# Attention in one fused network: a small product that gathers softmax denominators is given another place in TensorE's order

## The reference, cut to what matters

```python
q = jnp.einsum('qdh,bcd->bhcq', Q, x) * sq
k = jnp.einsum('qdh,bcd->bhcq', K, x) * sq
v = jnp.einsum('vdh,bcd->bhcv', V, x) * sv
att = jnp.einsum('bhcq,bhCq->bhcC', q, k) / d_query
att = jnp.where(causal, att, -jnp.inf)
p = jax.nn.softmax(att, axis=-1)
y = jnp.einsum('bhcC,bhCv->bhcv', p, v)
z = jnp.einsum('dvh,bhcv->bcd', W, y) * (...)
```

## Time and profile before

| | |
|---|---|
| median of three runs | 2140.64 us (2138.8 to 2143.95) |
| the profiled execution, its own time | 2142.65 us |
| its span in the profile | 2140.9 us |
| TensorE busy | 1889.4 us, 88% of the span |
| VectorE, ScalarE, GpSimd busy | 64%, 50%, 55% |
| attention, 650 to 1890 us of the span | TensorE busy 1216.50 of 1240 us |

### The profile page before, as it was taken

One profiled execution on the slowest core, in us unless ns is written; L12 is line 12 of the kernel. 1 busy time (PEld: TensorE's weight loads), 2 busy tenths in 40 slices (PEclk: granted clock), 3 DMA queues, 4 the chain that ended last, 5 costly groups with the idle time before them and its releaser, 6 DMA issues. The chain is left out here.

```text
span 2140.9 us, 39708 instructions
## 1 busy us (share of the span) xinstructions
PE 1889.4 (88%) x12071; PEld 1430.0 (67%) x12072; DVE 1361.5 (64%) x3652; ACT 1079.1 (50%) x2250; POOL 1177.9 (55%) x1159
## 2 busy tenths in 40 slices
PE   5864999999589999999999999999999999973870
PEld 3553888888466677777777677777777777753750
DVE  7884334434467777657777656777656777653763
ACT  5331333333455556646655646655646655522760
POOL 4364223223216666636687836687836687835782
PEclk9856999999899999999999999999999999977995
DMA  9853433333332111111221111121112111122979
GB/s 335 268 188 119 89 52 49 52 52 49 77 92 56 53 55 49 54 32 53 54 77 41 48 33 53 51 53 47 48 27 59 48 52 51 39 94 70 205 129 257
DMA packets 215682, 177.33 MB, mean 83 GB/s; under 512 B 85442, under 2 KB 200727, under 8 KB 214880
## 3 DMA queue, kind: packets, MB, share of 16 engines
q1 hardware_dynamic: 177904, 138.78, 22.1%
q0 software_dynamic: 28656, 27.61, 8.4%
q10 hardware_dynamic: 8960, 8.92, 1.2%
HBM read 95.05 MB, written 80.72 MB: 82 GB/s over the span
## 5 line engine op out<-in xcount | busy, mean ns | idle before, releaser
L952 POOL TENSOR_TENSOR c_den_late<-c_den_late,c_p 128x512 f32<-128x512 f32 (+3 forms) x384 | 409.9, 1068 | 227.6 <-ACT c_p L1267 183.5
L1267 ACT ACTIVATE c_p<-PS 128x512 f32<-128x512 f32 (+3 forms) x768 | 343.6, 491 | 196.1 <-PE PS L2483 119.0
L2452 PE MATMUL PS<-c_k,c_q 128*128 128x512 f32 (+2 forms) x768 | 289.3, 377 | 18.1 <-DVE c_max L1838 6.7
L2495 PE MATMUL PS<-c_p,c_vh 128*64 128x256 f32 (+3 forms) x3072 | 292.5, 333 | 0.0
L2475 PE MATMUL PS<-c_q,c_k 128*128 128x512 f32 (+2 forms) x768 | 283.7, 373 | 1.8 <-DMA c_q<-c_mr 1.2
L888 POOL DMA_INDIRECT acc<-b_y,b_tok x71 | 110.5, 1557 | 272.8 <-ACT b_y L1137 241.7
L2495 PEld LDWEIGHTS PS<-c_p,c_vh 128*64 128x64 f32 x3072 | 194.6, 137 | 96.0 <-issue 38.1
L2476 PE MATMUL PS<-c_q,c_k 128*128 128x512 f32 (+2 forms) x768 | 258.4, 348 | 0.0
L1258 ACT ACTIVATE c_q<-PS 64x512 fp32r<-64x512 f32 x256 | 151.0, 590 | 208.6 <-PE PS L2439 205.4
L1845 DVE CUSTOM_DVE_ANT_0 PS<-PS,c_maskq,c_max 128x128 f32<-128x128 f32 (+3 forms) x256 | 143.1, 559 | 105.5 <-PE PS L2452 71.5
L1838 DVE TENSOR_REDUCE c_max<-PS 128x1 f32<-128x512 f32 x256 | 175.5, 685 | 54.2 <-PE PS L2452 53.6
(11 more groups left out here) (304 smaller groups left out, 4009.7 us busy)
## 6 DMA issues: line engine op xcount, KB each, us to landing
c_vh<-c_v SPq DMA_DIRECT2D x64, 256.0 KB, 3.2
c_rrow<-rden SPq DMA_DIRECT2D x63, 256.0 KB, 3.6
routed<-b_empty SPq DMA_DIRECT2D x32, 289.0 KB, 10.2
d_xe<-routed SPq DMA_DIRECT2D x32, 289.0 KB, 4.0
b_xt<-routed SPq DMA_DIRECT2D x71, 130.0 KB, 2.1
b_w12T<-in_w12T_dram SPq DMA_DIRECT2D x16, 512.0 KB, 13.9
d_acc<-acc SPq DMA_DIRECT2D x16, 512.0 KB, 9.0
c_st_hi<-wqk_split SPq DMA_DIRECT2D x48, 128.0 KB
```

Of the source, the lines that this page charges most:

```text
L952: pool.tensor_tensor(den[:, off:], den[:, off:], p, ALU.add).then_inc(s_cPa, 1)
L1267: act.activation(c_p[:, P_AT[h][m]:P_AT[h][m] + WIDTH[m]], PS[:, ST_BANK[m % STB], skip:skip + WIDTH[m]], ACT.Exp, scale=ATT_SCALE).then_i ...
L2452: pe.matmul(PS[:, 2 + use[0], 0:max(w, 256)], c_q1[h][:, t * P:(t + 1) * P], c_k1[h][:, c * 512:c * 512 + max(w, 256)], start=True, stop=T ...
L2495: ins = pe.matmul(dst, c_vh[h][:, j, :], columns[:, :, a, :], start=(j == 0), stop=(t0 == 3))
```

## The change

`denominators(H - 1)` leaves its place between the seventh and the eighth of the `maxima` products and is put directly ahead of `outputs_of(0)`. In ordinary heads it comes later by two steps of the projections, by two z units in the second head of a pair, and by one `maxima` product. In `fetch` heads it comes earlier, ahead of `outputs_of(0)` instead of behind it. VectorE's list follows: `invert` is put behind `maximum(8)` in ordinary heads, and ahead of `maximum(7)` in `fetch` heads. No instruction is added or taken away.

```diff
@@ VectorE: head_steps
                 if fetch:
                     low_xT(b + 1, 0, table)
+                if fetch:
+                    invert(H - 1, 1 - h)
                 maxima(7)
-                if hd:
-                    invert(H - 1, 1 - h)
                 if h == 1 and zs:
                     add_z(b, pair - 1, (2, 3), table)
                 maxima(8)
+                if hd and not fetch:
+                    invert(H - 1, 1 - h)
                 routing(1)
@@ TensorE: head_products
                 if fetch:
                     transpose_x(b + 1, 0, table)
+                    denominators(H - 1, 1 - h)
                     outputs_of(0)
-                    maxima(7)
-                    denominators(H - 1, 1 - h)
-                    maxima(8)
+                    maxima(7, 8)
                 else:
                     projections(0)
                     maxima(7)
-                    if hd:
-                        denominators(H - 1, 1 - h)
                     projections(1)
                     if h == 1:
                         z_units(2, 3)
                     projections(2)
                     maxima(8)
+                    if hd:
+                        denominators(H - 1, 1 - h)
                     outputs_of(0)
```

## The result

The changed kernel takes 2137.22 us, the median of 20 runs (2131.44 to 2141.86); the kernel before took 2141.19 us in 20 runs beside it (2137.9 to 2145.65). The ratio is 0.9982, with a 95% interval of 0.9974 to 0.9991: about 3.9 us faster, between 1.9 and 5.6. The prediction said 12.3 us, and the measured time lies 0.7 us above its range.

The account below looks back on a forecast made before the run. TensorE's order was taken to bound attention (busy 1216.50 of 1240 us). 57 x 0.20 plus 3 x 0.4 less 3 x 0.1 made 12.3 us, from 2140.64 to 2128.3 us; range 2119 to 2136.5.

Parts of the forecast that it names:

- The saving per head: TensorE around denominators and `outputs`: 0.11 for a hidden load plus 0.095, about 0.20 us in each of 57 heads.
- The switch from 32 to 64: TensorE from denominators into `outputs`: taken as 0.09 us for the switch and 0.05 for loading 64 columns.
- the free switch: Rival: going from 32 to 64 columns on TensorE costs nothing, saving 0.34 us per head, 2120.3 us; chance 0.19.
- What moves later: Later denominators, 1.2 or 2.9 us: delays on GpSimd, VectorE's `invert`, SyncE and `outputs_of(1)` stay hidden in ordinary heads.
- I count these heads as +0.1 each with no saving: Three first-batch heads with row statistics on VectorE: 0.1 us longer each, 0.3 us in all.
- 0.22 short of `maximum(9)`: VectorE in those three heads: row statistics end at about 711.67, read as 0.22 us before `maximum(9)`.
- The shift: VectorE in the three heads: row statistics begin and end about 0.25 us later, `maximum(9)` at about 712.0.
- `fetch` heads: Three heads where denominators move ahead of `outputs`: TensorE's 0.48 us idle at `maxima(7)` goes, about -0.4 us each on top.
- Seven other heads: Heads 8 and 13 of the last three batches and the last but one: predicted -1.4 us together.
- the rival of absorption: Saving turns into TensorE waits for VectorE's row maxima; two thirds lost gives about 2137 us; partly absorbed, chance 0.04.
- Slower by VectorE's chain: Rival: inversion between `maximum(8)` and `maximum(9)` holds up VectorE's maxima; with no slack 45 us, 2186 us; chance 0.06.
- nothing comes of it: Rival: saving becomes waits for row maxima because VectorE sets the pace, within 4.3 us, at most 2140.6; chance 0.11.

Follow-up runs that it names:

- Experiment 6: Changed kernel with the row statistics moved late and, in ordinary heads, denominators one product earlier, ahead of maxima 8; ratio 1.0016 to the kernel before.
- experiment 8: Changed kernel with nothing moved, the two copies behind the row statistics written as reductions; 2133.37 us against 2139.86 for the kernel before, ratio 0.9970.
- Experiments 3: Changed kernel with only the two copies of the row statistics (means, variances) moved behind the query/key splits; ratio 0.9944 to the kernel before.
- experiment 5: Kernel before, with two awaited fills of a scratch tile ahead of the row statistics in three heads; 2164.00 us against 2156.58, ratio 1.0029.
- experiment 2: Kernel before, with only the row statistics moved behind maxima 10 and 11 and the splits; ratio 0.9996.
- experiment 1: Changed kernel with late statistics: row statistics moved behind maxima 10 and 11 and the splits; 2129.63 us against 2143.48 for the kernel before, ratio 0.9938.
- experiment 4: Changed kernel, but in the three heads with row statistics VectorE inverts behind them instead of in front; ratio 0.9948 to the kernel before.

## Why the prediction was right and wrong

*The saving per head: right.* Predicted 0.20 us, from 0.11 for the exposed weight load and 0.095 for the switch; measured 0.185 in 46 heads. The weight loads' "issue" wait at the projections, 10.9 us in 55 places before, is gone. Experiment 6 puts the two terms back by parting the neighbours again. *The switch from 32 to 64*: taken at 0.09 plus 0.05, measured at 0.10, and the free switch is refuted. The rule of the Trainium skill ("TensorEngine Tiling (Array Packing)", Key Properties) that changing the tiling mode drains TensorE, weighed in the prediction, agrees with these 0.10 us.

*What moves later: right for GpSimd, SyncE and `outputs_of(1)`.* GpSimd's wait grew to 105.9 us in 37 places (I had said over 100 in more than 45) and cost nothing; its waits for `c_p` shrank from 182.5 to 91.1 us. VectorE waits at line 1850 in only 4 places, not in most heads: maximum 8 ends about when the denominators are there.

*The step that failed*: "I count these heads as +0.1 each with no saving." The three heads with row statistics cost 2.2 each, 6.7 instead of 0.3. The slack was read wrong: "0.22 short of `maximum(9)`" was none. TensorE's product for maximum 9 ended at 672.89 in the first of these heads of the kernel before, 0.65 us ahead of the end of the copies (673.54), and the same 0.22 stands behind the copy in the changed kernel. So the statistics already held maximum 9 up, and every further delay there was bound to reach TensorE. That alone would have cost little: with the copies as reductions (experiment 8) the heads came out at +0.06 each, close to the +0.1. The shift was sized right: the statistics start 1.01 us behind `outputs` (667.45, 666.44) instead of 0.72 (671.46, 670.74), so 0.29 later where I had said 0.25. But I had followed only VectorE's own list. Of GpSimd I had asked whether its additions would be late, and not what of VectorE's would lie beside them. The copy had begun 0.17 us ahead of the addition; now it began 0.07 behind, where it waited for the whole of it. Experiments 3 and 8 show that the copies are the cause, experiment 5 that such a shift is enough. Of the 7.3 us that the three heads lost, 4.0 are TensorE's longer idle time and 3.3 the clock that fell behind it in two of them; the prediction had no term for either.

*`fetch` heads: wrong in size.* "About -0.4 each on top": they saved 0.14 each, not 0.6. TensorE no longer idles 0.48 us before `maxima(7)` but waits later, since the inversion (897.59 to 898.54 in the first of them) now stands in front of maximum 7 on VectorE instead of behind it. *Seven other heads* (8 and 13 of three batches, the last but one) gave nothing, together +0.7 instead of -1.4. The last but one head alone is 0.41 longer. It has no projections, and the denominators used to fill the time in which TensorE would have waited for VectorE ahead of `maxima(8)`; now TensorE idles 0.31 us there and makes the denominators afterwards. In head 8 TensorE waits longer at the twelfth maxima product for VectorE (the distance from the mask to it is 0.60 instead of 0.42), which is the rival of absorption on a small scale. I did not trace the rest.

*The signs of the rivals.* Slower by VectorE's chain: the chain of maxima was held up, but by a copy and not by the inversion, in three heads only. It took more than half of the gain. The time came out within the band of the rival "nothing comes of it" (within 4.3 us), though not by its mechanism alone.

*Open.* In the head-by-head sums the changed kernel gains 1.5 us in attention, while 20 runs a side say 3.9 (1.9 to 5.6). With late statistics the sums give 8.6 us against the trace of the kernel before and 9.8 against that of experiment 2, the runs 13 (10.5 to 16). Both sums leave out the first distance of all, which is 1.3 us longer in experiment 1 and 1.4 shorter in experiment 4 than before, though nothing in these kernels differs there. The traces are single executions, and the runs of one kernel differ by 6 to 13 us. Whether the remaining 2 to 4 us are a gain in a later stage or chance is not settled. Experiment 8 was measured on another chip than experiments 1, 3 and 4, and its interval overlaps that of experiment 4, so why it gains less is open as well.

## What to carry to other kernels

On a TensorE that never waits, read start against start. Here each change between divided and full width cost about 0.1 us and an exposed weight load behind it, so narrow products belong next to each other; that was worth 0.19 us per head, and 0.6% of the time once nothing else was hurt (experiment 1). When an edit shifts an engine's list by even 0.2 us, ask of each copy on VectorE which GpSimd operation it will now lie beside, and whether what stands behind it has any slack; the cheap mend is a gap with idle time for it, or a form that does not wait. An idle time of 0.22 us in front of an instruction was no such slack here: compare when its input was there with when the engine was free.

## What the runs showed of the hardware

- A copy of 128x4 numbers on VectorE took 1.25 us instead of 0.16 when a 1.28 us addition on GpSimd had begun 0.07 us before it; written as a reduction, in the same place, 0.15 us.
- The switch from 32 to 64 columns (0.10) and from 64 to 32 (0.10: 1396.28 to 1397.52 is 1.24, as long as with full width behind it) cost what each costs to and from full width.
- Idle times of 1.71 and 1.77 us on TensorE in an otherwise busy stretch were followed by the 1.2 GHz level in five of six cases (three heads each of the changed kernel and of experiment 5); in the same heads with at most 0.7 us of idle time (experiments 1, 3, 4 and 8) the granted clock of 640 to 740 us stayed at 1.00.
